# Run ends picked by one-hot products in the last edge stage of a graph network, and the third layer's gather buffers put away a turn sooner

## What is computed

```python
# third layer: softmax over the edges of one source, sum at the target
e = leaky_relu(ei_all[idx_i] + ej_all[idx_j], 0.01)
alpha = segment_softmax(e, idx_j)
out = relu(segment_sum(alpha[:, None] * x[idx_j], idx_i))

# fourth layer: per edge one of four relation matrices, maximum at the target
for r in range(4):
    msg = where(rel == r, x[src] @ weight[r] + bias[r], msg)
agg = segment_max(msg, dst)
h = x @ weight[-1] + bias[-1] + agg

x = layernorm(x + layer(x))          # after each layer
```

## Time and profile before

| what | value |
|---|---|
| median of three runs | 4120.34 us |
| the profiled execution | 4121.19 us |
| its span, first to last instruction | 4119.4 us |
[...]
| busy: GpSimd | 2912.2 us, 71% of the span |
| busy: TensorE matmul | 2465.8 us, 60% |
| busy: VectorE | 2245.0 us, 54% |
| busy: ScalarE | 1038.2 us, 25% |
| HBM | 147 GB/s over the span |

### The profile page before, as it was taken

The page is one execution under the profiler, slowest core; times in us unless marked ns, Lnnn a source line. Parts: engine busy times, 40 slices in busy tenths (PEclk is TensorE's granted clock), DMA queues, the critical chain, the costliest instruction groups (busy, mean ns, idle before and its releaser), DMA issues. The chain is left out here.

```text
span 4119.4 us, 67476 instructions
## 1 busy us (share of the span) xinstructions
PE 2465.8 (60%) x18096; PEld 2169.4 (53%) x18096; DVE 2245.0 (54%) x6458; ACT 1038.2 (25%) x2890; POOL 2912.2 (71%) x3009
## 2 busy tenths in 40 slices
PE   2566666676647777529999977777633333333330
PEld 2454555454436666529999976666523333333330
DVE  5777777777744444436767668876522222222224
ACT  0244454444410111114444411111111111111112
POOL 2777777777747777626777777777377777777775
PEclk8555655656658898655555557767756556555655
DMA  4344444444425666446666678787545455444443
GB/s 121 97 113 129 116 132 128 117 130 115 130 71 144 146 147 147 80 95 176 183 182 176 185 217 262 249 246 250 178 122 130 129 134 132 129 132 132 130 129 94
DMA packets 454541, 602.65 MB, mean 146 GB/s; under 512 B 112602, under 2 KB 322350, under 8 KB 451086
## 3 DMA queue, kind: packets, MB, share of 16 engines
q1 hardware_dynamic: 344578, 392.09, 31.1%
q0 software_dynamic: 95744, 198.37, 22.2%
q10 hardware_dynamic: 14000, 9.82, 0.8%
HBM read 420.34 MB, written 184.16 MB: 147 GB/s over the span
## 5 line engine op out<-in xcount | busy, mean ns | idle before, releaser
L628 POOL DMA_INDIRECT G<-table,IC x2096 | 2002.2, 955 | 743.7 <-issue 633.3
L3342 DVE TENSOR_TENSOR_SCAN GW<-BIG,GW,PS 128x512 f32<-128x512 bf16 x208 | 266.2, 1280 | 781.6 <-PE PS L3317 766.8
L3317 PE MATMUL PS<-IDENT,G 128*128 128x128 f32 x832 | 204.2, 427 | 679.3 <-DMA G<-table,IC 679.3
L2936 POOL DMA_INDIRECT G<-table,IC x448 | 465.6, 1039 | 196.4 <-issue 139.0
L3317 PEld LDWEIGHTS PS<-IDENT,G 128*128 128x128 f32 x832 | 162.8, 223 | 717.7 <-DMA G<-table,IC 520.7
L2936 POOL DMA_INDIRECT G<-table2c,IC x384 | 369.8, 963 | 123.5 <-issue 116.2
L1284 PE MATMUL PS<-SEL,GW 128*128 128x96 f32 x1664 | 371.7, 414 | 78.1 <-DVEq L1360 78.1
L1284 PEld LDWEIGHTS PS<-SEL,GW 128*128 128x128 f32 x1664 | 347.2, 318 | 118.2 <-DVEq L1360 118.2
L2950 PE MATMUL PS<-BIG 128*128 128x49 f32 x1680 | 377.5, 412 | 1.1 <-ACT BIG L2885 1.1
L2950 PEld LDWEIGHTS PS<-BIG 128*128 128x128 f32 x1680 | 371.3, 333 | 1.3 <-ACT BIG L2885 1.3
L1162 ACT CAST BIG<-PS 128x490 bf16<-128x490 f32 x288 | 199.8, 706 | 257.1 <-PE PS L1149 252.4
(11 more groups left out here) (378 smaller groups left out, 4525.7 us busy)
## 6 DMA issues: line engine op xcount, KB each, us to landing
rows_ahead<-G SPq DMA_DIRECT2D x104, 520.0 KB
running_max<-BIG SPq DMA_DIRECT2D x105, 512.0 KB
GW<-source_in_block SPq DMA_DIRECT2D x160, 256.0 KB
G<-table,IC POOLq DMA_INDIRECT x2544
SCRATCH<-rows_ahead SPq DMA_DIRECT2D x78, 520.0 KB
SCRATCH<-edge_places SPq DMA_DIRECT2D x209, 192.0 KB
edge_counts<-BIG SPq DMA_DIRECT2D x24, 1568.0 KB
BIG<-run_mask SPq DMA_DIRECT2D x104, 256.0 KB
```

What stands on the lines that cost most here:

```text
L628: pool.indirect_dma_start(out=G[:, b, u, 0:width], out_offset=None, in_=table, in_offset=bass.IndirectOffsetOnAxis(ap=IC[:, b * U + u:b * ...
L2936: pool.indirect_dma_start(out=GS[:, b, u, 0:width], out_offset=None, in_=table, in_offset=bass.IndirectOffsetOnAxis(ap=IC[:, b * U + u:b * ...
L3317: last = t.transpose(PS[2 * q + u // 4][:, (u % 4) * P:(u % 4 + 1) * P], G[:, b, u, 0:D], IDENT[:])
L3342: v.tensor_tensor_scan(RM[:, q, h * 512:(h + 1) * 512], MB[:, q, h * 512:(h + 1) * 512], PS[2 * q + h][:], before, ALU.min, ALU.max).then_ ...
```

## The change

In the third layer: in the first half all four buffers of a lap are put away within the lap (0 and 1 in its first turn, 2 and 3 in its second); 60 instead of 56 groups use the picked reciprocal; the planner starts from pair 26 at time 0 (PAIR * (pair - 26)) and ends with pair 49, since the last four groups are read straight from the gather buffers; the last three node blocks, and the load of the last layer's indices, are done at the end of the stage instead of in rest2, which is now a branch of the general path alone.

In the fourth layer: a new stage edges3_ends stands at the end of the list, taken when the flag for counted edges is set; edges3 and finish remain for the other case. It gathers, turns, scans, turns back and copies as before, but stores nothing to DRAM. A one-hot matrix that is 1 only where an edge is the last of its run picks those columns by a product, they are added into ACC at the window, and the finished node blocks (two every fourth group, as in the third layer) are turned, mixed, normalized and stored while the gathers go on.

```diff
@@ layer2: the third layer @@
-            PICKED = 56
+            PICKED = 60
+            KEEP = GROUPS - RING
-            for pair in range(26, GROUPS // 2):
+            for pair in range(26, KEEP // 2):
                 latest = (pair // 2, 1) if pair % 2 else (pair // 2 - 1, 3)
-                while points[place][0] < PAIR * (pair - 25) and points[place][1:] < latest:
+                while points[place][0] < PAIR * (pair - 26) and points[place][1:] < latest:
                     place += 1
+            def rows_of(i, b):
+                return GS[:, b] if i >= KEEP else LANDED[b]
+            def rows_wait(eng, i, turn, b):
+                if i >= KEEP:
+                    eng.wait_ge(gathered[b], turn * (16 * U) + 16 * U)
+                else:
+                    eng.wait_ge(landed[b], turn * 16 + 16)
@@ sp_group @@
+                if at >= KEEP:
+                    return
@@ sp_sums (and act_sums alike, with more_indices) @@
-                            if b == 1 and h == 0 and keep0:
-                                spill(sp, lap * 4 - 2, 2, lap - 1)
-                                spill(sp, lap * 4 - 1, 3, lap - 1)
-                            if b == 1 and h == 1:
-                                spill(sp, lap * 4, 0, lap)
-                                spill(sp, lap * 4 + 1, 1, lap)
+                            if b == 1:
+                                for slot in (2 * h, 2 * h + 1):
+                                    spill(sp, lap * 4 + slot, slot, lap)
@@ sync @@
-                        sp_sums(sp, reg, 0, 1, False)
-                        sp_sums(sp, reg, 1, LAPS // 2, True)
-                        spill(sp, 50, 2, 12)
-                        spill(sp, 51, 3, 12)
+                        sp_sums(sp, reg)
...
-                        sp.wait_ge(S.stored, 32 * CHUNKS + 32)
+                        sp.wait_ge(own_taken, PICKED)
+                        sp.dma_start(IDX3, IDX3D).then_inc(idx_in, 16)
+                        store_rows3(sp, S, CHUNKS, LEFT, NB - LEFT)
+                        sp.wait_ge(S.stored, 32 * CHUNKS + 32 + 16 * (NB - LEFT))
+                        sp.wait_ge(idx_in, 16)
@@ scalar, tensor, vector: the last three blocks follow in the stage @@
+                        act.wait_ge(acc_chain, GROUPS + 2)
+                        copy_sums(act, S, CHUNKS, LEFT, NB - LEFT, False)
+                        root(act, S, CHUNKS + 1, NB - LEFT)
+                        write_rows(act, S, CHUNKS, LEFT, NB - LEFT, X, False)
+                        copy_turned(act, S, CHUNKS, NB - LEFT)
...
+                        turn_sums(pe, S, CHUNKS, NB - LEFT, False)
+                        turn_rows(pe, S, CHUNKS, NB - LEFT)
+                        relations(pe, S, CHUNKS, NB - LEFT)
...
+                        mix_weighted(dve, S, CHUNKS, LEFT, NB - LEFT)
+                        scales(dve, S, CHUNKS + 1, CHUNKS, NB - LEFT)
+                        keep_relations(dve, S, CHUNKS, LEFT, NB - LEFT)
@@ rest2: every engine's part under "if is_general"; edges3 and finish: under "if not_counted" @@
+                    with pe.If(not_counted(pe)):
...
@@ edges3_ends, new @@
+                        for i in range(GROUPS):            # SyncE
+                            load_mask(sp, i)
+                            n = event(i, 3)
+                            if n is not None:
+                                store_out(sp, n)
...
+                        for i in range(GROUPS + 1):        # ScalarE
+                            if i < GROUPS:
+                                b = i % RING
+                                act.wait_ge(turned, i + 1)
+                                a.copy(IC[:, b * U:(b + 1) * U],
+                                       IDX3[:, (i + RING) * U:(i + RING + 1) * U]).then_inc(ic_ready, 1)
+                            if i >= 1:
+                                copy_back(act, i - 1)
...
+                def pick(pe, i):
+                    q = i % 2
+                    pe.wait_ge(copied, i + 1)
+                    pe.wait_ge(sel_ready, i + 1)
+                    if i >= 1:
+                        pe.wait_ge(added, i)
+                    for u in range(U):
+                        last = t.matmul(PS[6][:, 0:W], RB[:, q, u, :], SEL[:, q, u, :], start=u == 0, stop=u == U - 1)
+                    last.then_inc(picked, 1)
...
+                        for i in range(GROUPS + 1):        # TensorE
+                            if i < GROUPS:
+                                turn_in(pe, i)
+                            if i >= 1:
+                                turn_back(pe, i - 1)
+                            if i < GROUPS and event(i, 0) is not None:
+                                turn_nodes(pe, event(i, 0), i - 1)
+                            if i >= 1:
+                                pick(pe, i - 1)
+                        turn_nodes(pe, CHUNKS, GROUPS)
...
+                def select_ends(dve, i):
+                    if i >= 2:
+                        dve.wait_ge(picked, i - 1)
+                    v.tensor_tensor(SEL[:, i % 2], times(IOTA[:, 0:W], U), per(ENDREL[:, i * U:(i + 1) * U], W),
+                                    ALU.is_equal).then_inc(sel_ready, 1)
...
+                def add_ends(dve, reg, i):
+                    dve.wait_ge(picked, i + 1)
+                    if i >= 1:
+                        dve.wait_ge(added, i)
+                    w = window(dve, reg)
+                    v.tensor_tensor(ACC[:, ds(w, W)], ACC[:, ds(w, W)], PS[6][:, 0:W], ALU.add).then_inc(added, 1)
...
+                        for i in range(GROUPS + 1):        # VectorE
+                            if event(i, 2) is not None:
+                                scale(dve, event(i, 2))
+                            if i < GROUPS:
+                                dve.reg_load([regs[i % 2]], BASE[0:1, i:i + 1])
+                                select_ends(dve, i)
+                                scan(dve, i)
+                            if i >= 1:
+                                add_ends(dve, regs[(i - 1) % 2], i - 1)
+                            if i < GROUPS and event(i, 0) is not None:
+                                mix_best(dve, cn, event(i, 0))
+                        mix_best(dve, cn, CHUNKS)
+                        scale(dve, CHUNKS)
```

More of the change, by code:

```diff
@@ L2807, in sp_group, with sp_sums @@
                                  .to_broadcast([P, L])).then_inc(lo_in[1 - b % 2], 16)
-            def sp_sums(sp, reg, first, end, keep0):
-                with sp.Fori(first, end) as lap:
+            def sp_sums(sp, reg):
+                with sp.Fori(0, LAPS // 2) as lap:
                     for h in range(2):
@@ L2966, in pe_group @@
                     pe.wait_ge(sel_ready, i + 1)
[L2967 removed]
+                    rows_wait(pe, i, turn, b)
                     pe.wait_ge(added, i + 1)
                     for u in range(U):
[L2970 removed]
+                        last = t.matmul(PS[q][:, 0:W], rows_of(i, b)[:, u, 0:D], SEL[:, q, u, :],
                                         start=u == 0, stop=u == U - 1)
@@ new lines, in _ @@
+                    with dve.If(not_counted(dve)):
+                        v.memset(GW[:], 0.0).then_inc(chain, 1)
+                        dve.wait_ge(chain, 1)
+                        dve.sem_inc(scanned, 2)
+                        dve.sem_inc(zeroed, 1)
+                        with dve.Fori(0, LAPS) as turn:
+                            for b in range(RING):
+                                i, q = turn * RING + b, b % 2
+                                dve.wait_ge(turned, i + 1)
+                                dve.wait_ge(mask_in[q], (turn * 2 + b // 2) * 16 + 16)
+                                dve.wait_ge(back, i + 1)
+                                for h in range(2):
+                                    before = RM[:, 1 - q, L - 1:L] if h == 0 else RM[:, q, L // 2 - 1:L // 2]
+                                    dve.wait_ge(chain, i * 2 + h + 1)
+                                    v.tensor_tensor_scan(RM[:, q, h * 512:(h + 1) * 512],
+                                                         MB[:, q, h * 512:(h + 1) * 512], PS[2 * q + h][:],
+                                                         before, ALU.min, ALU.max).then_inc(chain, 1)
+                                dve.wait_ge(chain, i * 2 + 3)
+                                dve.sem_inc(scanned, 1)
@@ new lines, in turn_in, with turn_back @@
+                def turn_in(pe, i):
+                    b, q = i % RING, i % 2
+                    pe.wait_ge(gathered[b], i // RING * (16 * U) + 16 * U)
+                    if i >= 2:
+                        pe.wait_ge(scanned, i - 1)
+                    for u in range(U):
+                        last = t.transpose(PS[2 * q + u // 4][:, (u % 4) * P:(u % 4 + 1) * P], G[:, b, u, 0:D], IDENT[:])
+                    last.then_inc(turned, 1)
+                def turn_back(pe, i):
+                    q = i % 2
```

(38 more changed lines are left out.)

452 lines of the change are left out of this document (296 added, 156 removed).

## The result

The changed kernel takes 4106.35 us (median of six runs, 4100.66 to 4110.94), the kernel before beside it 4120.49 us (4117.63 to 4122.26): ratio 0.9967, 95% interval 0.9954 to 0.9979. That is faster by 14 us, where 36 us were forecast: inside the range of 4048 to 4112, but with less than half of the gain. The profiled execution took 4105.65 us for a span of 4103.8, against 4119.4 before, so the traces hold 15.6 us of difference.

A forecast was written before the change was run, and what follows sets the result against it. GpSimd's indirect gathers were taken to bound the last edge stage, VectorE the third layer's end. Terms -68.4 + 12 + 11 + 9 = -36.4 us gave 4084 us, range 4048 to 4112.

The forecast's parts named there:

- Gathers beside the comparison: Last edge stage: the comparison with both inputs in SBUF lengthens GpSimd's gathers, 12 us more.
- Rival (b): Last edge stage: the comparison hits the gathers harder, 31 us instead of 12, 4103 us; chance 0.15.
- Last window: Third layer: VectorE's last window addition comes 11 us later, between 12 us sooner and 20 us later.
- GpSimd's lead: Third layer, entering the second half: group 56's first gather starts sooner, near 2422.7 instead of 2434.93, by 12.2 us.
- the fallback: Third layer, second half: put-away points tied to GpSimd's gathers make the half fall back once by about 8 us.
- The extra picked turn: Third layer, second half: one more turn with picked reciprocal, 22.9 instead of 17.2 us; 3 of 5.7 us counted.
- Rival (a): Third layer: GpSimd's lead removes SyncE's waits, last window 12 us sooner instead of 11 later, 4061 us; chance 0.20.
- Seam: Third layer's last window to the last edge stage's first gather: 37.4 against 28.2 us, 9 us more.
- five skipped stages: Seam: again2, rest2, edges3, exact3 and finish are stepped through without work, costing 16.5 us.
- End: Last edge gather to span end: stage finish and its 49 gathers go, 24.5 against 92.9 us, 68.4 us less.
- rival c: Last edge stage: TensorE's in-order round outlasts the gathers; at 10.6 us a group 62 us more, 4146 us; chance 0.07.
- Rival (d): Last edge stage: the new stage is not entered and the old ones run, about 4120 us; chance 0.01.

The follow-up runs named there:

- the first experiment: Changed kernel with the last stage's comparison reading the node numbers from a copy in PSUM instead of SBUF: 4073.77 us, ratio 0.9891.
- the third experiment: Changed kernel with the planner placing put-aways at 20.3 us x (pair - 25) instead of (pair - 26): 4089.96 us, ratio 0.9932.
- pair - 25: Changed kernel with the planner one pair later: 4089.96 us; also with PSUM comparison, 56 picked groups, last group turned back first: 4052.98 us.
- pair - 24.5: Changed kernel with PSUM comparison, 56 picked groups, last group turned back first, planner at 20.3 us x (pair - 24.5): 4050.27 us, ratio 0.9841.
- the old third layer in the same session: Changed kernel with third layer and rest stage as before, PSUM comparison, last group turned back first: 4057.69 us, ratio 0.9858.
- The fifth experiment: Changed kernel without the five stages this input does not enter between third layer and last stage: 4093.82 us, ratio 0.9941.

## Why the prediction was wrong in size

**Gathers beside the comparison, 12 us forecast, 24.8 measured.** This is the step that failed most. The mechanism was the one named, its price was not. I scaled a mean of other work (37 ns over 49 gathers, for 26 us of such operations) by busy time, and took 12 between 7 and 31. What counts is how often a gather's start falls into a comparison and what is left of it then. With a comparison of 0.96 us and a start every 1.25 us that is 0.77 starts a group with 0.48 us left on average, if they fall at random: 0.37 us a group, 38 us in all, and 29 us with the 0.13 us taken off each that the first experiment shows (estimates). Measured were 94 hits of 0.25 us, 24 us. The lower end "they may fall in step" did not come: 94 of 104 comparisons were hit. Rival (b), 31 us, was the better number for this term.

A gather took 975 ns on average with both inputs of the comparison in SBUF, and 945 in the first experiment, with one in PSUM. Which part of a gather is held up, no run here separates.

**Last window, 11 us forecast, 19.6 measured.** Right: the points move one pair (20.3 us) and GpSimd's lead is less. Wrong: the lead, 7.0 us instead of 12.2, because the put-away of group 52 released its buffer 11.7 us behind its issue; I had carried 5.9 over from the earlier trace rows. Its two issues took 4.23 us, with four loads issued in the 6 us ahead of it, where those at 2429.04 before took 0.84 us behind three loads; that the loads delay it was not tried. So the fallback is 13.3 us instead of 8, and 13 to 15 us are what the mixing rows of most turns show (2605.19 to 2620.02, 2709.57 to 2722.47). The extra picked turn cost all of its 5.7 us, where I had counted 3: behind it the mixing rows are 18 to 20 us later. 13.3 and 5.7 are 19.0 of the 19.6 us, and the third experiment took 14.1 of them back with one number.

Rival (a), that GpSimd's lead pays, is borne out by no run. The change as made had 7 us of lead and lost; the kernels with the points at pair - 25 have none (10.9 and 10.6 us from the first comparison to group 56, 11.5 before). The best one, pair - 24.5, starts group 56 at 20.4 us, 9 us later than before, and its second half is still 8.9 us shorter than before, 525.6 us (8.2 less than with the old third layer in the same session). So that gain comes from later points, from the last four groups read in place, or both. The old third layer with later points is the rival that was not run, and by whole times the two kernels' intervals overlap.

**Seam, 9 us forecast, 4.9 measured.** I priced five skipped stages at 16.5 us by subtraction from another seam. Left out, they give 9.5 us. The rest of the seam is 23.6 us, 2.7 more than the 20.9 of the forecast, so part of the error was hidden by another. The fifth experiment has 1.9 us for each stage, its jump, barrier and semaphores included; their shares are not shown.

**End, -68.4 us forecast, -64.9 measured.** Two things were missing, and some were better. The order of TensorE's stream: the products of the group before stand between the scans and the transposes back, 3.7 us (4083.5 to 4087.23). The clock: the last products took 3.73 us instead of 2.5. In four runs of the new end they took that, at a granted clock of 0.50, with 28 us behind the last gather; in two they took 2.02 us, at 1.00, with 23.4. Against that the landing took 3.0 us instead of 4.0, and the node blocks and the last store were a little shorter (the last store's issue to the end of the span took 3.6 us instead of 4.5).

**TensorE's round (rival c)** did not decide: GpSimd's idle time stayed 0.30 us per gather with "issue" as its only cause, and TensorE itself still waited for landed gathers (1.73 us at 4067.42, while gathers were still being issued). **Rival (d)**: no row of finish is in the profile after.

## What to carry to other kernels

Price a held-up issue by its collisions, not by a share of busy time: how often the start of one operation falls into the other, and how much of it is then left (here 94 starts, 0.25 us each). Where two engines share a plan with assumed times, do not move the plan by more than the lead that is really there: here it was moved by 20.3 us for a lead of 7.0, and that cost 14 us. And where a stream of indirect gathers sets the time, try keeping one input of a large VectorE operation in PSUM: here one copy in the prologue was worth 25 us.

## What the runs showed that was not expected

A comparison of 128x768 with both inputs in SBUF delays only gathers that start inside it, by what is left of it less 0.13 us, 0.25 us on average; two of them in a row cost 1.4 times one (36.9 against 25.6 us of excess), not twice. The chip of the second session took 5570 us for a program that takes 4116 to 4120 us elsewhere; there the idle time of GpSimd ahead of its gathers grew, while a gather itself kept its 947 ns. Its cause stays open.
